# Last node stage of a two-layer graph network: rows that cross partitions mended in HBM, two tiles to a TensorE pass, rounds of eight

## The reference

```python
edge_index = jnp.stack([src, dst])
h = jnp.maximum(_layernorm(x, axis=-1), 0.0)
x = x + _L0_gnn_ref(edge_index, edge_type_2, h, ...)
h = jnp.maximum(_layernorm(x, axis=-1), 0.0)
x = x + _L1_gnn_ref(h, edge_index, edge_attr_32, ...)
...
row, col = (edge_index[0], edge_index[1])
qk_ij = jnp.sum(queries_i * keys_j, axis=-1)
alpha = segment_softmax(qk_ij, row, n)
...
msg_j = lin(W_v[:, None, :] * h_values[col], wvl_w, wvl_b)
aggr = jax.ops.segment_sum(alpha[:, :, None] * msg_j, row, num_segments=n).reshape(n, H)
out = lin(x, cen_w, cen_b) + aggr
return lin(ssp(out), out_w, out_b)
```

## Time and profile before

| what | before |
|---|---|
| median of three runs | 5188.86 us (5185.83 to 5190.13) |
| profiled execution, its own time | 5188.35 us |
| its span, first to last instruction | 5186.5 us |
| busy PE / DVE / ACT / POOL over the span | 55% / 74% / 54% / 64% |
| mean granted TensorE clock | 0.53 of full speed |
| last stage (from DVE's first instruction there) | 5023.5 to 5186.5 us |

### The profile page before, as it was taken

How to read it: one execution, slowest core, us unless ns; L and a number is a source line. 1 busy time by engine, 2 the same in 40 slices (tenths; PEclk the granted TensorE clock), 3 DMA queues, 4 the chain that set the end, 5 groups by cost and what they waited for, 6 DMA issues and landing times. The chain is left out here.

```text
span 5186.5 us, 79200 instructions
## 1 busy us (share of the span) xinstructions
PE 2840.6 (55%) x21444; PEld 1755.7 (34%) x21445; DVE 3846.0 (74%) x8928; ACT 2821.3 (54%) x5478; POOL 3293.8 (64%) x3386
## 2 busy tenths in 40 slices
PE   7777777777777777727777533333333333333335
PEld 7644444444444444417776311111111111111124
DVE  8999988888888888837876266666666666666654
ACT  4166666666666666612223366666666666666633
POOL 0167777777777777774001477777777777777762
PEclk9555555555555555557776555555555555555555
DMA  5222222222222222227662344444444444444421
GB/s 71 61 79 85 85 85 85 85 85 85 85 83 78 84 85 85 82 70 154 126 126 43 94 117 120 122 116 123 123 123 123 123 123 121 116 120 118 120 64 21
DMA packets 669069, 505.15 MB, mean 97 GB/s; under 512 B 566237, under 2 KB 583005, under 8 KB 668868
## 3 DMA queue, kind: packets, MB, share of 16 engines
q1 hardware_dynamic: 550868, 246.86, 19.9%
q0 software_dynamic: 108640, 196.86, 13.0%
q10 hardware_dynamic: 9360, 59.56, 3.0%
HBM read 289.86 MB, written 213.16 MB: 97 GB/s over the span
## 5 line engine op out<-in xcount | busy, mean ns | idle before, releaser
L612 POOL DMA_INDIRECT records<-rec,place x1612 | 1554.8, 965 | 745.8 <-issue 467.4
L1324 POOL DMA_INDIRECT got_a<-kv_table,idx_a x1612 | 1561.9, 969 | 501.8 <-issue 488.5
L849 DVE SCALAR_TENSOR_TENSOR same_before<-p_src,src_f,before 128x128 bf16<-128x128 f32 x1612 | 773.1, 533 | 0.0
L1340 PE MATMUL p_a<-ident,flat_attr 128*128 128x128 f32 x434 | 123.4, 431 | 832.5 <-ACT flat_attr L1377 790.5
L698 ACT ACTIVATE lo_away<-p_lo,minus_number 128x512 bf16<-128x512 f32 x434 | 285.2, 657 | 444.5 <-PE p_lo L653 444.5
L655 PE MATMUL p_src<-fields,select 3*128 3x512 bf16 x434 | 250.0, 576 | 402.7 <-DVE same_before L849 402.3
L1349 PE MATMUL p_a<-relu,w_t 128*128 128x512 f32 x248 | 230.9, 1035 | 419.3 <-DVE relu L1459 363.9
L994 PE MATMUL acc<-high,lo_r 128*128 128x64 bf16 x1708 | 344.5, 244 | 124.6 <-issue 87.2
L640 PE MATMUL p_h<-window,dst_hot 128*128 128x64 bf16 x4836 | 330.5, 239 | 146.0 <-ACT h_gated L717 123.2
L630 PE MATMUL p_look<-table_low,lo_hot_t 128*128 128x98 bf16 x1612 | 410.0, 281 | 0.0
L630 PE MATMUL p_look<-table_rest,lo_hot_t 128*128 128x98 bf16 x1612 | 409.4, 280 | 0.0
(11 more groups left out here) (361 smaller groups left out, 8575.6 us busy)
## 6 DMA issues: line engine op xcount, KB each, us to landing
sums<-packed_a ACTq DMA_DIRECT2D x62, 936.0 KB, 3.9
q_starts<-zero_q SPq DMA_DIRECT2D x62, 884.0 KB
rec_r<-records SPq DMA_DIRECT2D x124, 442.0 KB, 5.1
qin<-q_starts SPq DMA_DIRECT2D x62, 884.0 KB, 6.9
attr_a<-records SPq DMA_DIRECT2D x62, 442.0 KB, 5.0
records<-rec,place POOLq DMA_INDIRECT x1612
got_a<-kv_table,idx_a POOLq DMA_INDIRECT x1612
stage<-in_edge_attr SPq DMA_DIRECT2D x61, 416.0 KB
```

The lines of the kernel that those rows point to most:

```text
L612: nc.gpsimd.indirect_dma_start(k.records, bass.IndirectOffsetOnAxis(ap=place[b][:, t:t + 1], axis=0), rec[b][:, t, :], None).then_inc(s_se ...
L849: last = v.scalar_tensor_tensor(same_before[:, first:first + j + 1, :].rearrange("p g e -> p (g e)"), p_src[:, 0:(j + 1) * P], k.src_f[:, ...
L1324: nc.gpsimd.indirect_dma_start(got[b][:, t, :], None, k.kv_table, bass.IndirectOffsetOnAxis(ap=idx[b][:, t:t + 1], axis=0)).then_inc(s_got ...
```

## The change

In the last stage the tails are no longer spread over all nodes. Each partition finds at most one row to be mended: the sum of its own first node, if that began in an earlier partition (`came_on`) and ends in this one. It gathers that row (`fix`), takes the earlier partitions' part by one product of `heir` (a 128 x 128 matrix, which partition's last node is my first one) by `pay`, merges them, and scatters the result back to `sums1` (`fixed` to `fix_to`); partitions with nothing to mend write to 128 spare rows behind the table. The 49 gathers are issued after that scatter has landed. Then there is no merging per tile; `divided` only divides.

The rounds are now six of eight tiles and one of one. Two tiles (128 columns) are transposed at once, and multiplied by a 128 x 128 weight with the 64 x 64 block twice on its diagonal. On each engine steps of round r stand between steps of round r-1. The sum `xs` plus `out_br`, before in seven pieces, is one instruction over all 49 tiles.

To find the rows, `relation_nodes` stores `last_at` to a table `last_table` (6272 entries of four bytes) and POOL gathers each first node's entry into `fix_at`; three small DVE steps for `own_at` go. `attention_layer` gets eight small DVE steps that compute `fix_to`, ahead of its first chunk, and one store of zeros to the spare rows, ahead of its first load on SP. `front` loads the second copies of the weight blocks (five more transfers). Two semaphores become common to several stages, `s_passed` and `s_steps`.

```diff
 # front, SyncE and VectorE
-                    for w, to in (... (k.out_w, k.out_t[:])):
+                    for w, to in (... (k.out_w, k.out_t[0:D, 0:D]), (k.out_w, k.out_t[D:P, D:P])):
                         load(to, w.rearrange("o i -> i o"))
...
+                        again = slice(D + hd * HD, D + (hd + 1) * HD)
+                        load(k.vl_t[again, again], k.vl_w.rearrange("o i -> i o"))
 # relation_nodes, SyncE and GpSimd
+                    sp.dma_start(by_node(k.last_table), k.last_at[:].unsqueeze(2)).then_inc(s_ends, 16)
...
+                pool.wait_ge(s_ends, 16)
+                pool.wait_ge(s_first, 2)
+                pool.sem_inc(k.s_passed, 1)
+                nc.gpsimd.indirect_dma_start(
+                    k.fix_at[:], None, k.last_table,
+                    bass.IndirectOffsetOnAxis(ap=first_i[:, 0:1], axis=0)).then_inc(s_init, 16)
                 for hi in range(HI):
                     pool.wait_ge(s_kvq, hi + 1)
 # attention_layer, SyncE
+                sp.wait_ge(s_mend, 1)
+                sp.dma_start(k.sums1[STREAM:STREAM + P, :], spare[:]).then_inc(s_spare, 16)
                 loop(sp, body)
 # attention_nodes, GpSimd
+                nc.gpsimd.indirect_dma_start(
+                    fix[:], None, k.sums1, bass.IndirectOffsetOnAxis(ap=k.fix_at[:, 0:1], axis=0)).then_inc(s_fix, 16)
+                pool.wait_ge(s_fixed, 1)
+                pool.sem_inc(k.s_passed, 1)
+                nc.gpsimd.indirect_dma_start(
+                    k.sums1, bass.IndirectOffsetOnAxis(ap=k.fix_to[:, 0:1], axis=0), fixed[:], None).then_inc(s_sent, 16)
+                pool.wait_ge(s_sent, 16)
+                pool.sem_inc(k.s_passed, 1)
+                for r, (a, b) in enumerate(rounds):
+                    for hi in range(a, b):
                         nc.gpsimd.indirect_dma_start(
                             sums[:, hi, :], None, k.sums1, ...).then_inc(s_sums[r], 16)
 # attention_nodes, TensorE
+                for r in range(R + 1):
+                    if r < R:
+                        turn(0, r, u, s_u)
+                    if r >= 1:
+                        turn(1, r - 1, z, s_y)
+                    if r < R:
+                        apply(0, r, k.vl_t, s_z)
+                    if r >= 1:
+                        apply(1, r - 1, k.out_t, s_x)
 # attention_nodes, ScalarE: copy(0, r), copy(1, r - 1), then
+                    if r < R:
+                        act.wait_ge(s_z, r + 1)
+                        c.then(nc.scalar.activation(soft[:, rr, :], z[:, rr, :], ACT.Abs))
+                        c.then(nc.scalar.activation(soft[:, rr, :], soft[:, rr, :], ACT.Exp, scale=-1.0))
+                        nc.scalar.activation(soft[:, rr, :], soft[:, rr, :], ACT.Ln, bias=half[:], scale=0.5).then_inc(s_soft, 1)
 # attention_nodes, VectorE
+                c.wait()
+                v.tensor_tensor(fixed[:, 0:QW], fix[:, 0:QW], part[:, 0:QW], ALU.add).then_inc(s_fixed, 1)
+                c.mark(v.tensor_tensor(k.xs[:], k.xs[:], bc(k.out_br[:], 1, HI), ALU.add))
...
+                def divided(r):
...
+                    dve.wait_ge(s_sums[r], 16 * (b - a))
+                    c.then(v.reciprocal(over[:, rr, :], den))
+                    c.then(v.tensor_tensor(over[:, rr, :], over[:, rr, :], bc(k.filled[:, rr], 2, NH), ALU.mult))
+                    v.tensor_tensor(u[:, rr, :]..., sums[:, rr, 0:D]..., bc(over[:, rr, :], 3, HD), ALU.mult).then_inc(s_u, 1)
+                    c.then(v.tensor_tensor(share[:, rr, :], den, over[:, rr, :], ALU.mult))
+                    c.then(v.tensor_tensor(soft[:, rr, :]..., bc(heads(k.vl_br[:]), 1, b - a), bc(share[:, rr, :], 3, HD), ALU.mult))
+                    c.then(v.tensor_tensor(k.centre[:, rr, :], k.centre[:, rr, :], soft[:, rr, :], ALU.add))
...
+                for r in range(R + 1):
+                    if r < R:
+                        divided(r)
+                    if r >= 1:
+                        activated(r - 1)
+                    if r < R:
+                        summed(r)
+                    if r >= 1:
+                        added(r - 1)
```

More of the change, by code:

```diff
@@ L1276, in attention_layer @@
         packed = [tile(f"packed_a{b}", [P, T, SW]) for b in range(2)]
+        mend = tile("mend", [P, 4])
+        spare = tile("spare", [P, SW])
         net_t = tile("net_t", [P, GROUPS * P])
@@ L1540, in attention_nodes @@
     nc = k.nc
-    R = 7
     W = SW + 1
-    assert HI % R == 0 and R * W <= 512
+    K = 8
+    rounds = [(a, min(a + K, HI)) for a in range(0, HI, K)]
+    R = len(rounds)
     with ExitStack() as ctx:
         tile, bank, sem = helpers(k, ctx)
-        own = tile("own2", [P, ROWS])
         sums = tile("sums_f", [P, HI, SW])
-        parts = tile("parts_f", [P, HI, W])
-        vals = tile("vals", [P, 2 + NH])
-        diag = tile("diag", [P, 2 + NH, P])
+        u = tile("u_f", [P, HI, D])
+        fix, fixed = tile("fix", [P, SW]), tile("fixed", [P, SW])
+        vals = tile("vals", [P, 3 + NH])
+        diag = tile("diag", [P, 3 + NH, P])
         peer = tile("peer", [P, P])
@@ L1554, in attention_nodes @@
         no_peer = tile("no_peer", [P, P])
+        heir = tile("heir", [P, P])
         top = tile("top_f", [P, NH])
@@ L1558, in attention_nodes @@
         pay = tile("pay", [P, W])
-        top_r, fac_e, fac_t, tmp = (tile(n, [P, HI, NH]) for n in ("top_r", "fac_e", "fac_t", "tmp_f"))
-        empty = tile("empty", [P, HI])
-        feat = [tile(f"feat_f{b}", [D, R * P]) for b in range(2)]
+        part = tile("part_m", [P, W])
+        new_top, factor = tile("new_top", [P, NH]), tile("factor_f", [P, 2, NH])
+        over, share = tile("over", [P, HI, NH]), tile("share", [P, HI, NH])
+        feat = [[tile(f"feat_f{a}{b}", [P, K // 2 * P]) for b in range(2)] for a in range(2)]
         z = tile("z", [P, HI, D])
@@ L1595, in _ @@
+                for r, (a, b) in enumerate(rounds):
+                    pool.wait_ge(s_sums[r], 16 * (b - a))
             @block.tensor
             def _(pe):
-                pe.wait_ge(s_made, 1)
-                nc.tensor.matmul(p_bc[0][:, 0:NH * P], k.ones[:], diag[:, 2:2 + NH, :].rearrange("p v k -> p (v k)"), start=True, stop=True)
-                nc.tensor.matmul(p_bc[1][:, 0:2 * P], k.ones[:], diag[:, 0:2, :].rearrange("p v k -> p (v k)"), start=True, stop=True).then_inc(s_bc, 1)
-                pe.wait_ge(s_made, 3)
@@ new lines, in apply @@
+                def apply(a, r, weight, read):
+                    pe.wait_ge(s_feat, count(a, r))
+                    if r >= 2:
+                        pe.wait_ge(read, r - 1)
+                    for j, n in pairs_of(r):
+                        last = nc.tensor.matmul(p_out[a][r % 2][:, j * D:(j + n) * D], feat[a][r % 2][0:n * D, j * D:j * D + P],
+                                                weight[0:n * D, 0:n * D], start=True, stop=True)
+                    last.then_inc(s_out, 1)
@@ L1651, in _ @@
[L1651 to L1660 removed]
+                        copy(0, r)
@@ L1673, in _ @@
+                c.mark(v.memset(half[:], 0.5))
                 dve.wait_ge(s_bc, 1)
-                c.then(v.tensor_scalar(peer[:], p_bc[1][:, 0:P], k.last_row[:], None, ALU.is_equal))
-                c.then(v.tensor_tensor(peer[:], peer[:], p_bc[1][:, P:2 * P], ALU.mult))
-                c.mark(v.tensor_tensor(peer_later[:], peer[:], k.less[:], ALU.mult))
+                c.then(v.tensor_scalar(peer[:], p_rows[:, 0:P], k.last_row[:], None, ALU.is_equal))
+                c.then(v.tensor_tensor(peer[:], peer[:], p_rows[:, P:2 * P], ALU.mult))
@@ L1683, in _ @@
                 v.tensor_scalar(shrink[:], shrink[:], 0.0, None, ALU.min).then_inc(s_exp_in, 1)
+                c.mark(v.scalar_tensor_tensor(heir[:], p_rows[:, 2 * P:3 * P], k.last_row[:], k.less[:], ALU.is_equal, ALU.mult))
+                c.then(v.tensor_tensor(peer_later[:], peer[:], k.less[:], ALU.mult))
+                c.then(v.tensor_reduce(later[:], peer_later[:], AX.X, ALU.add))
                 c.then(v.tensor_scalar(pay[:, SW:W], later[:], 0.0, None, ALU.is_equal))
@@ new lines, in _ @@
+                dve.wait_ge(s_part, 1)
+                c.then(v.tensor_copy(part[:], p_part[:, 0:W]))
+                c.then(v.tensor_scalar(later[:], part[:, SW:W], -1.0, FAR, ALU.add, ALU.mult))
+                c.then(v.tensor_scalar(part[:, QW:SW], part[:, QW:SW], later[:], None, ALU.add))
+                dve.wait_ge(s_fix, 16)
+                c.then(v.tensor_tensor(new_top[:], part[:, QW:SW], fix[:, QW:SW], ALU.max))
+                c.mark(v.tensor_tensor(factor[:, 0, :], fix[:, QW:SW], new_top[:], ALU.subtract))
@@ new lines, in _ @@
+                v.tensor_tensor(factor[:, 1, :], part[:, QW:SW], new_top[:], ALU.subtract).then_inc(s_exp_in, 1)
+                c.mark(v.tensor_copy(fixed[:, QW:SW], new_top[:]))
+                dve.wait_ge(s_exp_out, 2)
+                for a, of in enumerate((fix, part)):
```

(14 more changed lines are left out.)

266 lines of the change are left out of this document (116 added, 150 removed).

## The result

| | kernel before | changed kernel |
|---|---|---|
| time, median (range) | 5187.99 us (5185.83 to 5190.13, 4 runs) | 5128.23 us (5125.61 to 5129.31, 4 runs) |
| profiled execution: time, span | 5188.35, 5186.5 us | 5128.93, 5127.2 us |
| last stage, from DVE's first copy to the end of the span | 163.0 us | 103.5 us |

The ratio is 0.9884, 95% interval 0.9867 to 0.9901: 60 us less. The forecast was 5132.6, range 5123 to 5148. The last stage begins at 5023.70 in place of 5023.53 and gives back 59.5 us; nothing else moves the end.

A forecast was written before the change was run, and what follows sets the result against it. The last stage was taken as bound by its chain of waits, 17.25 us a round, no engine full. Head, POOL-paced rounds and 23.6 us tail end at 5130.3, from 5186.5; 5132.6 us in the median, range 5123 to 5148.

The forecast's parts named there:

- Head: Start of the last stage: serial path from 5023.5 through `peer` (5029.1) and the last `pay` (5033.8) to `fixed` at 5036.9.
- The scatter: POOL's write of mended rows: held by the 3.4 us `xs` sum plus 0.83, ending at 5041.1, about 4 us, not 0.95.
- a rival from the Trainium skill: Last stage's scatter: the `xs` sum does not hold it, gathers begin 3.2 us earlier, time 5129.5; 16%.
- the form of the operands: Last stage: the `xs` sum holds POOL because its operands are contiguous inside, like `own`; a sum of another shape holds nobody.
- First of the 49 gathers: Last stage, POOL: gathers begin at 5043.0, 18.9 us later than before, and the last is issued 60.0 us after the first.
- The rounds: Last stage: POOL's gathers at 1.25 us set the pace, rounds of eight 10.0 us apart, plus 0.4 for DVE holds.
- The loop: Last stage: the engines' chain through DVE and PE that must close in each round, 9.8 us, just under 10.0.
- the rival of 18%: Last stage: the engines' loop, not POOL, sets the rounds' pace; each us over 10.0 costs six, 5136 to 5155; 18%.
- No overlap: Last stage: engines do not overlap as ordered, the old 17.25 us a round stays, 43 us more, 5176; 3%.
- The tail: From the sixth round's rows (5106.7) to the end: 23.6 us, ending at 5130.3, including the one-tile round.
- The store of `last_table`: Layer 1's node stage: 6272 four-byte packets at 9.1 ns, 3.6 us, hidden by 18 us of room.
- the slower rival: Layer 1's node stage: that store runs on one engine and each write costs several times 9.1 ns; up to 5287; 2%.

The follow-up runs named there:

- Experiment 1: Changed kernel with the `xs` sum moved from right behind `fixed` to right behind `diag`, away from the scatter: 5125.11 us (kernel before 5187.3).
- experiment 3: Changed kernel without the scatter of mended rows, so the 49 gathers do not wait for it: 5114.98 us (kernel before 5187.3).
- experiment 2: Changed kernel with the `xs` sum in its old place but the tile index innermost, stride 256 bytes: 5134.02 us, one run.
- experiments 4: Changed kernel with rows from the second round on brought by six plain loads of consecutive rows, not gathers: 5119.50 us (kernel before 5187.3).
- experiment 10: Kernel with only the `xs` sum moved behind `diag`, plus POOL waiting each round until the previous round's rows landed: 5133.92 us (kernel before 5186.89).
- experiment 5: Changed kernel with the staggered order undone, each engine ending a round before the next: 6045.55 us where the kernel before takes 6081.16.
- experiment 7: Changed kernel with `last_table` stored four times and POOL waiting for all, run twice: 6021.52 us (before 6081.16) and 6036.15 (before 6082.72).
- experiment 8: Changed kernel with the one-tile round first, sizes 1, 8, 8, 8, 8, 8, 8: 6008.61 us where the kernel before takes 6081.16.
- the kernel with both changes: Changed kernel with the `xs` sum behind `diag` and the one-tile round first: 6006.87 us (before 6082.72); again, 5124.42 (before 5186.89).

## Why the prediction was right

Right in mechanism at each step of the main path, and 4.4 us high in the median. Of that 3.1 are in the trace (end at 5130.3, measured 5127.2), from terms that were nearly all a little high; the rest is that the profiled execution lies 0.7 above the median, where 0.5 below was taken. The terms did not make up for one another:

- *Head.* `peer` at 5028.6 (forecast 5029.1): right, `own` had hidden PE. `fixed` ended at 5036.0 (5036.9): the last `pay` was 0.8 sooner, and the small steps with the exponent took 2.2 from `part_m` on, not 2.5. The start's 0.4 was 0.2, less than executions differ by; the attention layer's load came 0.3 later.
- *The scatter.* Held until 0.87 after the `xs` sum (forecast 0.83). Experiment 1 shows the cause, experiment 3 repeats it with a gather. This was the step with a rival from the Trainium skill ("SBUF — State Buffer", Who interferes with whom), by which descriptor generation is not stalled by `tensor_tensor`: the runs speak against it, 3.35 us beside the sum and 1.00 without. My reason why differs, the form of the operands, is wrong (experiment 2): that product reads one operand from PSUM, and the sums and products that held POOL read both from SBUF.
- *First of the 49 gathers* at 5042.2 (5043.0), their spread 61.18 us: 1.2 us over 60.0, where I had put 2.4. Last full round's rows at 5104.55 (5106.7).
- *The rounds.* 10.15 to 10.42 apart (10.0 plus 0.4), paced by POOL: experiments 4 and 10. The loop was 9.15 (9.8), so the rival of 18% had 1.1 us of room against it, not 0.2. The largest of its misses are the products, 1.9 a kind where I had 2.2 twice.
- *No overlap* (3%): the order does what it says; experiment 5 prices it at some 33 us.
- *The tail.* 22.65 (23.6).
- *The store of `last_table`.* The mis-sized term: 24.8 us, not 3.6. I took the 9.1 ns of loads for a store of the same four bytes. The queue in the changed kernel, 2790 to 2820 us:

```profile
q1 hardware_dynamic: 6544, 0.03, 59.9%
```

  Worked as in the earlier trace rows, that is 44 ns of engine time a packet, and one engine alone would show 6% at most: dearer packets, as the slower rival said, but on all engines. The Trainium skill ("DMA: Bandwidth & Descriptors", Specifications) names a read-modify-write below 512 bytes. The trace agrees that the store is dear, with 24.8 us for 6272 packets; but the loads of the earlier trace rows are below 512 bytes as well, and no run shows the mechanism. It was still far below the room that the slower rival needed. But POOL's scatters did begin 4.2 us late, and that was hidden only because POOL later waits for `kvq` anyway: of the 22 us between the store's issue and POOL's first scatter nothing was left.

## What to carry to other kernels

A serial path in front of a paced stream costs about its length (12.6 us for 15.9 here), even though the other engines are half idle: look for the engine that is never free (POOL, 31.10 of 40.79 us busy and issuing in the rest), and move out of its way whatever holds it, here DVE instructions with both operands in SBUF. When a chain of four engines is staggered by one round, its worth is the chain less the slowest queue, here 16.0 against the 10.2 that POOL then sets; price both, and ask whose queue comes next (here the engines at 9.15). Read a queue's price for stores from stores, not from loads of the same size.

## What the runs showed of the hardware

- A DVE sum or product of two SBUF operands that is under way when POOL's indirect DMA begins holds it until 0.79 to 0.87 us after its own end, in scatters and gathers alike (3.35 and 6.50 us for 1.00, 4.15 for 0.94; 1.41 beside the product `u_f`), whatever the order of its elements. With one of the two operands in PSUM it does not: 418 gathers, none over 0.95 us.
- The same sum of 3136 columns takes 3.42 us with 4-byte steps inside and 6.65 us with 256-byte steps.
- POOL starts its scatter 0.85 us after the end of the DVE step that it waits for (5035.96 to 5036.82), and its first gather 0.77 to 0.81 after the landing.
- Products: 0.22 us a pass of 64 columns and 0.26 of 128 at a granted clock of 0.50, 0.24 of 128 at 0.65.
- Four stores of 6272 four-byte packets took 71.8 to 73.1 us, one 24.8: 44 ns of engine time a packet in the store, 9.1 in loads of four bytes.
- On the chips where before takes 6080 us, engines stood still for up to 43 us at a time in the last stage and in experiment 7's node stage, beginning inside POOL's long runs of indirect DMAs. Most of what such a chip loses lies ahead of that, in stages that were not read: in experiment 8 the last stage begins at 5863.13 us. In experiment 7 DVE did so for 24.29 us up to 3524.85, and POOL's run of scatters ended at 3523.9. In the last stage of the kernel with both changes, in order of time:

```profile
5947.78 0.69 DVE L1783 TENSOR_TENSOR z<-p_of,centre 128x512 f32<-128x512 f32 x1 [32.14 <-remote]
...
5949.73 0.94 POOL L1638 DMA_INDIRECT sums_f<-sums,last_at  x1 [0.30 <-issue]
```

  DVE stood still for 32 us and went on 2 us before POOL's last gather (the second row) began. No such stand still is in the last stage of any trace from the other chips. What the engines wait for, no run shows: experiment 10 was to tell, and fell on another chip.
